# First attention by four heads: one score matmul per block, rough scores two tiles at a time

## What is computed

```python
# NUM_HEADS = 16, HEAD_DIM = 8; query x (2, 512, 128), key = value = ctx_1024 (2, 154, 128)
q = (query @ Wq.T + bq).reshape(b, tq, 16, 8).transpose(0, 2, 1, 3)   # k, v alike
scores = einsum('bhqd,bhkd->bhqk', q, k) / sqrt(8)
attn = softmax(scores, axis=-1)
out = einsum('bhqk,bhkd->bhqd', attn, v)  ...  return out @ Wo.T + bo
```

## Time and profile before

| | |
|---|---|
| time, three runs | 280.88 us median, 279.95 to 281.87 |
| profiled execution | 281.86 us, its span 280.1 us |
| mean granted TensorE clock | 0.971 |
| PE busy | 241.9 us, 86% |
| VectorE, ScalarE, GpSimd busy | 179.9, 133.3, 72.3 us |
| first attention, first score to last attend | 22.4 to 81.1 us |

### The profile page before, as it was taken

The page is one execution under the profiler, slowest core; times in us unless marked ns, Lnnn a source line. Parts: engine busy times, 40 slices in busy tenths (PEclk is TensorE's granted clock), DMA queues, the critical chain, the costliest instruction groups (busy, mean ns, idle before and its releaser), DMA issues.

```text
span 280.1 us, 3659 instructions
## 1 busy us (share of the span) xinstructions
PE 241.9 (86%) x1235; PEld 166.0 (59%) x1244; DVE 179.9 (64%) x416; ACT 133.3 (48%) x268; POOL 72.3 (26%) x103
## 2 busy tenths in 40 slices
PE   6787999989987675999999768788889999999993
PEld 2353546454644322668788537665568888888872
DVE  2695435465437786877245173688888888888883
ACT  2534355654652870152444234766555555555551
POOL 2564060740115120000092030030023535253200
PEclk9999799999999888899999997999999999999998
DMA  7990000000000000000033000000002121210001
GB/s 239 419 354 0 2 0 0 4 0 1 0 2 0 0 0 2 1 0 2 0 92 100 0 0 0 2 0 1 0 2 68 45 75 41 75 39 0 2 0 75
DMA packets 4468, 11.52 MB, mean 41 GB/s; under 512 B 761, under 2 KB 1113, under 8 KB 4194
## 3 DMA queue, kind: packets, MB, share of 16 engines
q1 hardware_dynamic: 4146, 10.47, 11.4%
q10 hardware_dynamic: 304, 0.82, 0.9%
HBM read 10.77 MB, written 0.52 MB: 40 GB/s over the span
## 4 chain that ended last, share of the span: by engine, by line
PE 62%; DVE 16%; issue 8%; ACT 6%; POOL 5%; DMA 2%; ACTq 0%; DVEq 0%; POOLq 0%
PE bank L1508 5%; PE bank L1512 5%; PE bank L1509 5%; PE bank L1040 4%; PE bank L1113 3%; DVE att L567 3%; PE bank L1541 3%; DVE smax L471 3%; PE bank L1394 3%; PE bank L1538 3%; PE bank L1157 2%; PE bank L1384 2%; PE bank L1539 2%; PE bank L1521 2%; POOL arena_a L320 2%
## 5 line engine op out<-in xcount | busy, mean ns | idle before, releaser
L1005 ACT ACTIVATE arena_d<-bank,bias 128x512 f32<-128x512 f32 x34 | 23.4, 688 | 33.1 <-PE bank L1512 33.1
L861 ACT ACTIVATE arena_c<-bank 128x512 f32<-128x512 f32 x40 | 23.1, 598 | 23.0 <-PE bank L1144 23.0
L471 DVE TENSOR_REDUCE smax<-bank 128x8 f32<-128x1232 f32 x16 | 22.8, 1439 | 15.6 <-PE bank L1113 15.6
L732 DVE SCALAR_TENSOR_TENSOR arena_d<-bank,bias,arena_d 128x512 f32<-128x512 f32 x34 | 25.5, 750 | 10.5 <-ACT arena_d L1005 10.5
L1508 PE MATMUL bank<-arena_b 128*128 128x512 f32 x68 | 27.0, 396 | 0.3 <-DVE arena_d L741 0.3
L1512 PE MATMUL bank<-arena_b 128*128 128x512 f32 x68 | 26.5, 390 | 0.0
L1509 PE MATMUL bank<-arena_b 128*128 128x512 f32 x68 | 26.5, 389 | 0.0
L388 POOL CAST arena_b<-rec 128x512 fp32r<-128x512 f32 x17 | 13.5, 793 | 49.0 <-PE bank L1541 49.0
L295 POOL TENSOR_TENSOR rstd<-vareps,neghalf 128x4 f32<-128x4 f32 x8 | 8.1, 1011 | 63.2 <-DVE vareps L430 63.2
L746 DVE TENSOR_TENSOR arena_a<-arena_d,arena_a 128x512 fp32r<-128x512 f32 x34 | 23.2, 682 | 0.7 <-ACT arena_a L1012 0.7
L1012 ACT CAST arena_a<-arena_d 128x512 fp32r<-128x512 f32 x34 | 20.8, 610 | 3.6 <-DVE arena_d L741 2.2
(11 more groups left out here) (247 smaller groups left out, 511.3 us busy)
## 6 DMA issues: line engine op xcount, KB each, us to landing
rec<-in_rec SPq DMA_DIRECT2D x17, 257.0 KB, 2.7
arena_d<-in_fc SPq DMA_DIRECT2D x1, 2048.0 KB, 10.4
fc<-in_fc SPq DMA_DIRECT2D x1, 2048.0 KB, 14.8
x<-in_x SPq DMA_DIRECT2D x2, 256.0 KB, 5.5
out<-x SPq DMA_DIRECT2D x2, 256.0 KB, 2.0
pack<-in_pack ACTq DMA_DIRECT2D x1, 452.0 KB, 4.5
watt<-in_watt SPq DMA_DIRECT2D x1, 384.0 KB, 6.0
ctx<-in_ctx ACTq DMA_DIRECT2D x1, 308.0 KB, 6.5
```

Source lines behind the costliest of these rows:

```text
L471: dve.tensor_reduce(smax[:, n, :].rearrange("p (q h) -> p q h", q=2), heads(flat[:, c0:c0 + NBLK * P]), AX.X, ALU.max).then_inc(Z["max_don ...
L732: dve.scalar_tensor_tensor(to[:, k % 2, :], bank[:, 2 + k % 2, :], bias[:, u % SPLITS, 1:2], sil[:, k % 2, :], ALU.add, ALU.mult).then_inc ...
L861: act.activation(pT[:, n % RING, :], bank[:, 3 + n % 2, :], ACT.Exp, scale=float(DH) ** -0.5)\
L1005: act.activation(sil[:, k % 2, :], bank[:, k % 2, :], f, bias=bias[:, STEPS[k][0] % SPLITS, 0:1])\
```

## The change

The first attention works by quads, four heads of one batch (`cc`, 0 to 7; QW = 32 rows). Query and key are projected with weights that hold the 32 rows three times, so one copy gives all parts: rows 0-31, 32-63 and 64-95 of the query are high, low, high, of the key high, high, low. Four more rows carry the negated maximum against the head mask (the key tile is filled with ones there). So one matmul with 100 rows (`KQ`) makes a block's scores. All eight key expansions are kept (`ks`), each of 100 x 616, and six queries (`QSLOTS`). A rough call covers two tiles of 128 query rows with one quad, 2 x 616 columns in four matmuls, and one reduction takes both. The indicator load, its copies and the second query copy go; the weights are 1024 columns instead of 768; block order and placements are written anew, for each combination.

```diff
-ROUGH_AT = (1, 3, 5, 7)
-ORDER = (0, 3, 5, 8, 1, 4, 6, 9, 2, 7)
+ORDER = ((0, 3, 1, 4, 2, 5, 8, 6, 9, 7), (0, 3, 1, 4, 5, 8, 2, 6, 9, 7),
+         (0, 3, 1, 5, 8, 4, 6, 9, 2, 7), (0, 3, 1, 5, 8, 4, 6, 9, 2, 7))
 # GpSimd
+            pool.memset(kh[:, :, :, :].bitcast(F32), 1.0).then_inc(Z["pad_zero"], 1)
+            pool.memset(ks[:, :, HALF:].bitcast(F32), 0.0).then_inc(Z["pad_zero"], 1)
+            pool.memset(smax[:, :, :], 0.0).then_inc(Z["pad_zero"], 1)
-            for c in range(2, COMBOS):
-                pool.wait_ge(Z["score_psum"], (c - 1) * NBLK)
-                expand(ka, khi, c, P)
-                expand(kb, klo, c, HW)
+            expand(4)
+            expand(5)
+            values(1)
...
+            expand(6)
+            expand(7)
 # VectorE (k_lo and q_lo: 32 rows of the key, 308 columns; 32 rows of the query, 512)
+            k_lo(0)
...
+            dve.tensor_tensor(*expansion(0)).then_inc(Z["k_first"], 1)
+            k_lo(1)
             q_lo(0)
+            k_lo(2)
+            maxima(0, 0)
+            k_lo(3)
+            maxima(0, 1)
+            q_lo(1)
             dve.wait_ge(L["x1"], 16)
+            second = measure(x, TB)
+            maxima(1, 0)
+            maxima(1, 1)
+            center(second, x, xn, TB, "xn_ready")
+            q_lo(2)
...
+            maxima(2, 0)
+            q_lo(3)
+            maxima(2, 1)
+            maxima(3, 0)
+            q_lo(4)
+            maxima(3, 1)
+            q_lo(5)
+            maxima(4, 0)
+            normalise(0)
+            maxima(4, 1)
+            maxima(5, 0)
+            maxima(5, 1)
+            q_lo(6)
+            q_lo(7)
+            maxima(6, 0)
+            normalise(1)
+            maxima(6, 1)
+            maxima(7, 0)
+            maxima(7, 1)
 # ScalarE, behind exponential i of combination c
+                    if (c, i) in ((0, 5), (0, 8), (0, 9), (1, 1), (1, 9), (2, 1)):
+                        queries({(0, 5): 2, (0, 8): 3, (0, 9): 4, (1, 1): 5, (1, 9): 6, (2, 1): 7}[c, i])
 # TensorE
+            def rough(cc, p):
...
+                for t, parts in ((0, ((0, 512), (512, HALF))), (1, ((HALF, 1024), (1024, 2 * HALF)))):
+                    for k0, k1 in parts:
+                        ins = pe.matmul(flat[:, c0 + k0:c0 + k1],
+                                        qs[0:3 * QW, cc % QSLOTS, (2 * p + t) * P:(2 * p + t + 1) * P],
+                                        ks[0:3 * QW, cc, k0 - t * HALF:k1 - t * HALF], start=True, stop=True)
...
-                pe.matmul(bank[:, 3 + n % 2, :], ka[:, c % 2, cols], qa[:, c % 2, :], start=True, stop=False)
-                pe.matmul(bank[:, 3 + n % 2, :], kb[0:HW + HH, c % 2, cols], qb[0:HW + HH, c % 2, :],
-                          start=False, stop=True).then_inc(Z["score_psum"], 1)
+                pe.matmul(bank[:, 3 + n % 2, :], ks[0:KQ, cc, j * P:(j + 1) * P], qs[0:KQ, cc % QSLOTS, :],
+                          start=True, stop=True).then_inc(Z["score_psum"], 1)
...
+            early_work(4, 0)
+            rough(0, 0)
+            rough(0, 1)
+            keys(3)
+            queries(1)
+            maxima(0)
             for c in range(COMBOS):
                 for i in range(NBLK):
                     scores(c, i)
+                    if (c, i) in ((0, 8), (1, 7), (2, 6), (3, 6)):
                         attend(c, 0)
+                    if c == 0:
+                        if i in (0, 2):
+                            rough(1, i // 2)
+                        if i in (1, 3):
+                            values(0, i // 2)
+                        if i == 4:
+                            maxima(1)
+                            queries(2)
+                        if i == 5:
+                            turned(1)
+                        if i in (6, 8):
+                            rough(2, i // 2 - 3)
+                        if i == 7:
+                            queries(3)
+                        if i == 9:
+                            rough(3, 0)
+                            queries(4)
+                    if c == 1:
+                        if i == 0:
+                            queries(5)
+                        if i == 1:
+                            maxima(3)
+                        if i in (2, 4, 6, 8):
+                            rough(3 + (i + 2) // 4, i // 2 % 2 == 0)
...
+                    if c == 2:
+                        if i == 0:
+                            queries(7)
+                        if i in (1, 3, 5, 7):
+                            rough(6 + i // 4, i // 2 % 2)
+                        if i == 3:
+                            out_turned(1)
...
                 attend(c, 1)
+                if c == 0:
+                    rough(3, 1)
+                    maxima(2)
+                if c in (1, 2):
+                    maxima(2 * c + 2, both=True)
                 attend(c, 2)
```

More of the change, by code:

```diff
@@ L28 @@
 COMBOS = 2 * B
+HQ = HH // 2
+QW = HQ * DH
+KQ = 3 * QW + HQ
+QUADS = 2 * COMBOS
+QSLOTS = 6
 E0, F0 = 8, 512
@@ L839, in gate_rows @@
                 act.copy(srep[:, b * S:(b + 1) * S], bank[:, 3 + b, :]).then_inc(Z["srep_ready"], 1)
+            keys(0)
+            keys(1)
             turned(0)
             queries(0)
-            act.wait_ge(L["ind"], 16)
-            act.wait_ge(Z["pad_zero"], 2)
-            for n in range(2):
-                act.copy(kb[HW:HW + HH, n, :], ind).then_inc(Z["kb_ind"], 1)
+            keys(2)
+            act.wait_ge(Z["gsum_psum"], 1)
+            act.mul(gsum[:, :], bank[:, 5, 0:E0], 2.0).then_inc(Z["gsum_ready"], 1)
+            keys(3)
+            queries(1)
             indicators(act.copy, 0)
-            for r in range(2):
-                values(0, r)
-            act.wait_ge(Z["gsum_psum"], 1)
-            act.mul(gsum[:, :], bank[:, 7, 0:E0], 2.0).then_inc(Z["gsum_ready"], 1)
             minus_max(0)
@@ L1064, in _, with keys @@
             pe.wait_ge(L["watt"], 16)
-            for g in range(2):
-                pe.matmul(bank[:, 3 + g, 0:B * SK], watt[:, 2 + g, :], ctx2[:, :, 0:SK], start=True, stop=True)\
+            def keys(g):
+                if g == 3:
+                    pe.wait_ge(Z["klo_ready"], 3)
+                pe.matmul(keys_bank(g)[0:3 * QW, :], wk(g), ctx2[:, :, 0:SK], start=True, stop=True)\
                     .then_inc(Z["k_psum"], 1)
+            keys(0)
+            keys(1)
             pe.wait_ge(L["pack"], 16)
@@ L1126, in maxima @@
+            def maxima(cc, both=False):
+                pe.wait_ge(Z["max_done"], 2 * (cc + 1 + both))
+                if cc == 0:
+                    pe.wait_ge(Z["klo_ready"], 4)
+                else:
+                    pe.wait_ge(Z["mT_ready"], cc)
+                if cc >= 4:
+                    pe.wait_ge(Z["att_ready"], cc // 2 - 1)
+                q0, q1 = (0, QW + HQ) if both else (cc % 2 * QW, cc % 2 * QW + HQ)
                 for i in range(TB):
-                    ins = turn(bank[0:HH, 7, i * P:(i + 1) * P], smax[:, c * TB + i, :])
+                    ins = turn(bank[0:q1 - q0, 7, i * P:(i + 1) * P], smax[:, cc // 2 % 2 * TB + i, q0:q1])
@@ L1230, in _ @@
             queries(0)
-            early_work(8, 7)
-            for i in range(TB):
-                rough(0, i)
-                if 1 <= i < TB - 1:
-                    early_work(4, 7)
+            keys(2)
             pe.wait_ge(L["gate"], 16)
-            pe.matmul(bank[:, 7, 0:E0], neghalf[:, 0:1].broadcast_to([P, P]), gate[:, :], start=True, stop=True)\
+            pe.matmul(bank[:, 5, 0:E0], neghalf[:, 0:1].broadcast_to([P, P]), gate[:, :], start=True, stop=True)\
                 .then_inc(Z["gsum_psum"], 1)
-            for r in range(2):
-                values(0, r)
+            early_work(4, 0)
+            rough(0, 0)
+            rough(0, 1)
+            keys(3)
+            queries(1)
             maxima(0)
-            early_work(3, 5)
             for c in range(COMBOS):
@@ new lines, in _ @@
+                    if c == 1:
[6 more added lines that the diff above has]
+                        if i == 3:
+                            out_turned(0)
+                        if i in (5, 7):
+                            values(1, (i - 5) // 2)
+                        if i == 9:
+                            queries(6)
```

325 lines of the change are left out of this document (142 added, 183 removed).

## The result

The changed kernel took 286.84 us (286.69 to 289.4), the kernel before beside it 280.56 (279.95 to 281.87): ratio 1.0221, 95% interval 1.017 to 1.0273. It is slower, by about 6 us (4.8 to 7.7 by the interval), where 285.0 was forecast from a base of 280.88. The profiled execution took 286.93 us.

What follows compares the result with a forecast made beforehand. The first attention was taken to be driven by TensorE's work and the rough-score loop with VectorE, in strict queue order. Span 280.1 + 1.1 (order) + 3.0 (clock falls) = 284.2; on the median 285.0 us, 80% range 277 to 289.

Steps and rivals of the forecast that it cites:

- Ramp: Stretch up to the first attention's first score matmul: claimed to end at 19.4 us, a gain of 3.0 us.
- c0: First combination (batch and head half), now six rough calls instead of four: claimed 22.5 us, ending at 41.9 instead of 40.6.
- c1: Second combination, with four rough calls and two values groups: claimed 14.8 us, against 15.1 before.
- the walk: Instruction-by-instruction tracing of the first attention's new queue order with fixed durations: stage end 82.0 us, +1.1 without clock change.
- bank 6: In c0, the second batch's transposes need this bank, freed by queries 2's low part: TensorE stands from 26.3 to 28.65.
- c2: Third combination, where a low part and a normalisation stand ahead of reductions: claimed 16.1 us instead of 14.0.
- c3: Last combination, without rough calls: claimed 9.2 us, against 11.4 before.
- Rough in four pieces: Rough scores made by four matmuls instead of three: claimed 0.93 us from start to reduction, against 0.87.
- The clock: TensorE's longer pauses in the first attention bring three more falls to half speed, 1.0 us each: +3.0 us.
- No more falls: Rival: the clock holds, or slow passes lie under VectorE's reductions; +1.1, 282.0 us; chance 0.27.
- The halved scores: First attention's removed score passes, 9.4 us of PE work, as shadow work beside the loop; part of the forecast, same price.
- The faster rival: Waits inside c0 and c2 are shorter, so these keep 18.2 and 14.0 us: 275.4 us; chance 0.20.

Runs made afterwards that it cites:

- warm: The changed kernel with 43 filler matmuls writing to an idle bank, placed where TensorE waits in the first attention; 280.84 us, ratio 1.0002.
- c0_order: The changed kernel with only the order inside c0 changed, on TensorE, ScalarE and VectorE; 282.42 us, ratio 1.0025.
- turn_bank7: The changed kernel with the second batch's transposes written to bank 7 instead of bank 6, no operation moved; 283.06 us, ratio 1.0074.
- dve_order: The changed kernel with four moves on VectorE: two query low parts and two normalisations placed behind maxima; 282.52 us, ratio 1.007.
- orders_no_fill: The changed kernel with the new order inside c0 and the four VectorE moves, without fillers; ratio 0.9728, resting on two executions.
- all_three: The changed kernel with the new order inside c0, four moves on VectorE and 13 filler matmuls; 272.78 us, ratio 0.9676.
- before_warm: The kernel before with ten filler matmuls in c0, where TensorE stood before its one clock fall in this stage; 280.85 us, ratio 1.0002.
- double_pass: The changed kernel with every score matmul of the first attention made twice, with the same operands; 293.32 us, ratio 1.0384.

## Why the prediction was right

*Ramp.* Forecast first score 19.4, measured 19.17. The low part of a key cost 0.54 where 0.5 was estimated. The 0.15 us for the larger weights wasn't needed: the key projection began at 7.56 (7.68 before).

*c0.* The forecast's late steps are the measured ones, in the same order: transposes at 28.65 (29.35), rough (3,0) at 36.9 (38.40), c1 at 41.9 (44.90). In warm, with a full clock, they came at 28.13, 36.11 and 41.04, so the delays are the clock's, and the walk itself was 0.5 to 0.9 us too slow. c0_order shows that the order, and not the amount of work, made c0 long. Naming bank 6 as what holds PE was half right: turn_bank7 frees the bank, and rough (2,0) still waits for low part 2. *c1* 14.8 forecast, 14.7 measured. *c2* 16.1, in warm 15.4, under the fall 17.85; dve_order confirms the two operations that stood ahead of ready reductions. *c3* 9.2, measured 9.24.

*Rough in four pieces.* From its start to the reduction the forecast took 0.93 us; in the changed kernel a rough at 49.99 is reduced from 50.93, one at 52.43 from 53.35.

*The clock.* Three more falls were counted at the pauses of the walk, and three came, at those places; that they came is in part chance, since dve_order, c0_order and turn_bank7 had pauses of 1.8 to 2.55 us without a fall. Their price was mis-sized: 1.0 us each, 3.0 in all, where warm gives back 6.1 us for the four. Pairs of profiles give 1.2 to 1.5 us for one short fall (dve_order against the changed kernel in c0, orders_no_fill against all_three, before_warm against before) and 2.4 for the long one in c2. The estimate priced one slow rough and one step more; slow attends, queries and transposes stand on the path as well. And one fall was left out of the sum: it was called "already in the time before", but the walk, which replaced that time, was at full clock and held none. The walk erred the opposite way: it ended the stage at 82.15, and warm ends at 80.4. So the forecast stands on a right mechanism and on two misses that partly cancel: +4.1 forecast for the span, +5.0 measured. The case for *No more falls* misread its rows: between first score and last attend of the kernel before PE has one pause of 1.72 us and no other over 0.61, not several of 1 us.

*The halved scores.* The text called them shadow work beside the loop. That was too strong: they are worth about half of their length, 4 to 5 us, in the old order, in the new one and with the waits out. In the changed kernel that gain is inside its +6 us; without it the loss would be larger, as double_pass shows. *The faster rival* asked for a c1 before 38.5. all_three has it at 36.5 and is faster than before: the mechanism was right, the change as written didn't reach it.

## What to carry to other kernels

Work taken from the fullest engine pays only as far as its waits go too: walk each queue in program order with measured durations, and look at what stands ahead of an operation whose input is ready. When TensorE is left with pauses of two microseconds, expect falls of its clock behind them, not in every execution, and price a fall with everything slow that stands on the path: here 1.2 to 1.5 us for a short one. A sum that replaces a measured stretch by a walk at full clock has to put all falls back in. Test the idea and its order apart: here the same 40 fewer matmuls gave 2.2% slower or 3.2% faster, by the order inside c0, four moves on VectorE and 13 filler matmuls (2.7% without these). And compare stages as well as whole times: the time alone made the same pass look three times dearer in one order than in another.

## What the hardware showed beside that

In the changed kernel's profile TensorE's pauses of 1.79, 2.04 and 2.53 us, and a pair of 2.22 and 1.79, were each followed by a fall to 0.50, which lasted 3.2 to 3.6 us, and 6.5 behind the pair. Pauses as long stayed without one elsewhere: 1.79 us in dve_order and c0_order, at the very place where the changed kernel had its first fall, and 2.55 in turn_bank7. So pause length alone doesn't decide it in these traces; what else does wasn't tested. Execution times go with the mean granted clock: dve_order took 280.79 us at 0.972 and 287.85 at 0.946. Where the clock is held in the stage, times scatter less: warm's ten from 279.7 to 281.42, all_three's four from 272.06 to 273.32, against 280.5 to 287.85 for dve_order.
